# Moving the row sums, the roots and a weight staging inside the slots of a quantised attention stage

## What is computed

```python
x_int = x_int - jnp.max(x_int, axis=-1, keepdims=True)
x_int = jnp.maximum(x_int, n * x0_int)            # n = 30
q = jnp.floor(x_int / x0_int)
r = x_int - x0_int * q
z = r * (r + b_int) + c_int
exp_int = jnp.maximum(jnp.floor(z * jnp.exp2(n - q)), 0.0)
exp_sum = jnp.sum(exp_int, axis=-1, keepdims=True)
ratio = jnp.round(exp_sum / jnp.maximum(exp_int, 1.0))
big = jnp.floor(jnp.log2(ratio))
big = big + jnp.where(ratio - jnp.exp2(big) >= jnp.exp2(big - 1.0), 1.0, 0.0)
out = jnp.exp2(-jnp.clip(big, 0.0, qmax - 1.0))
```

## Time and profile before

| what | value |
|---|---|
| median of three runs | 658.2 us |
| the profiled execution, its own time | 656.87 us |
| its span in the profile | 655.1 us |
| DVE busy | 535.2 us, 82% of the span |
| ACT busy | 443.7 us, 68% |
| POOL busy | 402.9 us, 62% |
| PE busy | 369.4 us, 56% |
| attention slots 0 to 24 | about 74 to 413 us of the span |

### The profile page before, as it was taken

How to read it: one execution, slowest core, us unless ns; L and a number is a source line. 1 busy time by engine, 2 the same in 40 slices (tenths; PEclk the granted TensorE clock), 3 DMA queues, 4 the chain that set the end, 5 groups by cost and what they waited for, 6 DMA issues and landing times.

```text
span 655.1 us, 13415 instructions
## 1 busy us (share of the span) xinstructions
PE 369.4 (56%) x3593; PEld 236.0 (36%) x3593; DVE 535.2 (82%) x1380; ACT 443.7 (68%) x782; POOL 402.9 (62%) x450
## 2 busy tenths in 40 slices
PE   0598254072452633534536221278979999999264
PEld 0144112031130311312313111256757777777153
DVE  3688699679898897798998989669769998988566
ACT  0046657478767677677686765376878899998753
POOL 9773433431546487586785885477777777777600
PEclk9999555555555555555555555578989999999679
DMA  8546997786959969743422432466467776682098
GB/s 196 67 64 179 366 279 154 257 250 209 304 124 335 226 205 324 154 102 85 114 53 61 101 73 64 107 147 135 116 142 141 124 136 137 137 143 60 14 390 306
DMA packets 191976, 107.76 MB, mean 164 GB/s; under 512 B 137746, under 2 KB 186011, under 8 KB 191906
## 3 DMA queue, kind: packets, MB, share of 16 engines
q1 hardware_dynamic: 181634, 89.22, 56.2%
q0 software_dynamic: 10272, 17.70, 8.8%
HBM read 23.61 MB, written 60.67 MB: 129 GB/s over the span
## 4 chain that ended last, share of the span: by engine, by line
PE 27%; DVE 23%; SPq 13%; issue 13%; DMA 12%; ACT 8%; POOL 2%; DVEq 0%; POOLq 0%; ACTq 0%
PE pS L1925 8%; DMA pTs<-S_p 5%; PE pP L1925 5%; SPq L523 5%; PE pX L1943 4%; DVE S_e L1497 3%; DVE negmx L1422 3%; PE pO L1943 3%; SPq L611 2%; DMA w2s<-expert_rows 2%; SPq L514 2%; PE pS L1666 2%; DMA arena<-in_x_dram 2%; PE pS L1668 2%; DMA bias_rows_hl<-bias_hl 2%
## 5 line engine op out<-in xcount | busy, mean ns | idle before, releaser
L836 POOL DMA_INDIRECT expert_rows<-stage,dest x118 | 124.0, 1051 | 37.3 <-issue 29.6
L765 POOL DMA_INDIRECT region<-rows,slots x60 | 73.7, 1228 | 23.5 <-issue 16.3
L758 POOL CAST arena<-arena 128x384 bf16<-128x384 int8 x42 | 27.0, 643 | 70.0 <-ACT arena L926 69.3
L1843 PE MATMUL pP<-WpT,oq 128*128 128x192 bf16 x72 | 15.9, 359 | 74.0 <-ACT oq L1025 69.2
L1710 PE MATMUL pX<-arena,WA 128*128 128x384 f16 x86 | 34.9, 509 | 39.1 <-ACT arena L926 28.2
L765 POOL DMA_INDIRECT region<-arena,slots x36 | 45.5, 1265 | 18.4 <-issue 11.2
L926 ACT ACTIVATE arena<-pX,qkB,qkA 128x384 int8<-128x384 f32 x43 | 28.4, 661 | 41.6 <-PE pX L1710 41.6
L664 POOL TENSOR_TENSOR w1s<-stage,w1s 128x768 f16<-128x768 f32 (+1 forms) x16 | 33.8, 2113 | 32.9 <-ACT w2s L912 32.3
L1856 PE MATMUL pO<-pTs,vq 88*32 88x96 bf16 (+1 forms) x576 | 12.5, 238 | 71.5 <-DMA pTs<-S_p 71.3
L1497 DVE SCALAR_TENSOR_TENSOR S_e<-S_sq,kf,S_pow 128x1056 f32<-128x1056 f32 x24 | 38.2, 1591 | 16.7 <-ACT S_sq L1039 16.6
L1011 ACT ACTIVATE S_g<-S_w,kf 128x1056 int16<-128x1056 uint16 x24 | 30.3, 1264 | 27.7 <-DVE S_w L1427 27.7
(11 more groups left out here) (428 smaller groups left out, 1434.6 us busy)
## 6 DMA issues: line engine op xcount, KB each, us to landing
region<-zrow SPq DMA_DIRECT2D x11, 3200.0 KB, 12.2
w1s<-expert_rows SPq DMA_DIRECT2D x16, 384.0 KB, 8.0
stage<-in_L_ffn_w_dram SPq DMA_DIRECT2D x16, 192.0 KB
stage<-in_L_ffn_w_dram SPq DMA_DIRECT2D x32, 96.0 KB
w2s<-expert_rows SPq DMA_DIRECT2D x8, 384.0 KB, 11.7
arena<-in_x_dram SPq DMA_DIRECT2D x4, 672.0 KB
expert_rows<-stage,dest POOLq DMA_INDIRECT x118
out_dram<-xsel SPq DMA_DIRECT2D x8, 198.0 KB
```

Source lines behind the costliest of these rows:

```text
L765: pool.indirect_dma_start(region_rows, bass.IndirectOffsetOnAxis(ap=slots[q % 3][:, i, m:m + 1], axis=0), rows[q % 3][:, i, :].bitcast(I16 ...
L836: pool.indirect_dma_start(y_dram, bass.IndirectOffsetOnAxis(ap=dest[(st - 7) % 8][:, j:j + 1], axis=0), ysb[b][:, j, :], None, bounds_chec ...
```

## The change

On DVE the exponentials S_e of tile n - 1 stand at the head of slot n, followed by `top_experts` of the slot before and the maximum of tile n, and their sums stand behind that maximum. On ACT the root and its square stand together at the head of slot n and are written to a new tile S_y; the square over S_rho stands ahead of `scale_pair` and `split_pair`. The ratio reads S_y. Semaphores and their counts follow.

```diff
+        S_y = sb("S_y", [128, H, KEEP], F32)
...
@@ ACT, slot @@
+                if 1 <= st <= NT:
+                    act.wait_ge(s["e_ready"], n)
+                    if st >= 2:
+                        act.wait_ge(s["ratio_ready"], n - 1)
+                    act.activation(S_y[:, :, :], S_e[:, :, :], ACT.Abs_reciprocal_sqrt,
+                                   bias=k(K_TINY)).then_inc(s["inv_root"], 1)
+                    act.wait_ge(s["inv_root"], n)
+                    act.activation(S_y[:, :, :], S_y[:, :, :], ACT.Square).then_inc(s["y_ready"], 1)
                 if st < NT:
...
                     quant_qk(q + 1, 3, fill(st, "qk", 3))
+                if st < NT:
+
+                    act.wait_ge(s["rho_ready"], n + 1)
+                    if st >= 1:
+                        act.wait_ge(s["e_ready"], n)
+                    act.activation(S_sq[:, :, :], S_rho[:, :, :], ACT.Square, bias=k(K_NB2)).then_inc(s["sq_ready"], 1)
                 if i == 2 and st <= 20:
                     scale_pair(q + 1)
                 if i == 0 and 3 <= st < NT:
                     split_pair(q)
-                if st < NT:
-
-                    act.wait_ge(s["rho_ready"], n + 1)
-                    if st >= 1:
-                        act.wait_ge(s["ratio_ready"], n)
-                    act.activation(S_sq[:, :, :], S_rho[:, :, :], ACT.Square, bias=k(K_NB2)).then_inc(s["sq_ready"], 1)
...
-                if st < NT:
-
-                    act.wait_ge(s["e_ready"], n + 1)
-                    act.activation(S_sq[:, :, :], S_e[:, :, :], ACT.Abs_reciprocal_sqrt,
-                                   bias=k(K_TINY)).then_inc(s["inv_root"], 1)
                 if nxt and i < 2:
                     quant_qk(q + 1, 5 * i, fill(st, "qk", 5 * i))
-                if st < NT:
-                    act.wait_ge(s["inv_root"], n + 1)
-                    act.activation(S_sq[:, :, :], S_sq[:, :, :], ACT.Square).then_inc(s["y_ready"], 1)
...
@@ DVE, slot @@
+                if 1 <= st <= NT:
+
+                    dve.wait_ge(s["sq_ready"], n)
+                    dve.wait_ge(s["pow_ready"], n)
+                    dve.wait_ge(s["inv_root"], n - 1)
+                    dve.wait_ge(s["sum_ready"], n - 1)
+                    dve.scalar_tensor_tensor(S_e[:, :, :], S_sq[:, :, :], k(K_KK), S_pow[:, :, :].bitcast(BF16), ALU.add,
+                                             ALU.mult).then_inc(s["e_ready"], 1)
+                if 0 < st <= NT and quad_at(st - 1, GATE) is not None:
+                    top_experts(quad_at(st - 1, GATE))
                 if st < NT:
                     dve.wait_ge(s["u_ready"], n + 1)
                     dve.wait_ge(s["w_ready"], n)
                     dve.tensor_reduce(negmx[:, :], S_u[:, :, :], AX, ALU.max, negate=True).then_inc(s["max_ready"], 1)
+                if 1 <= st <= NT:
+                    dve.wait_ge(s["e_ready"], n)
+                    dve.wait_ge(s["ratio_ready"], n - 1)
+                    dve.tensor_reduce(esum[:, :], S_e[:, :, :], AX, ALU.add).then_inc(s["sum_ready"], 1)
+                if st < NT:
...
-                                             S_sq[:, :, :], ALU.max, ALU.mult).then_inc(s["ratio_ready"], 1)
+                                             S_y[:, :, :], ALU.max, ALU.mult).then_inc(s["ratio_ready"], 1)
...
-                if st < NT:
-
-                    dve.wait_ge(s["sq_ready"], n + 1)
-                    dve.wait_ge(s["pow_ready"], n + 1)
-                    dve.wait_ge(s["inv_root"], n)
-                    dve.wait_ge(s["sum_ready"], n)
-                    dve.scalar_tensor_tensor(S_e[:, :, :], S_sq[:, :, :], k(K_KK), S_pow[:, :, :].bitcast(BF16), ALU.add,
-                                             ALU.mult).then_inc(s["e_ready"], 1)
-                    dve.wait_ge(s["e_ready"], n + 1)
-                    dve.wait_ge(s["ratio_ready"], n)
-                    dve.tensor_reduce(esum[:, :], S_e[:, :, :], AX, ALU.add).then_inc(s["sum_ready"], 1)
-                if quad_at(st, GATE) is not None:
+                if quad_at(st, GATE) is not None and st >= NT:
                     top_experts(quad_at(st, GATE))
```

## The result

The changed kernel takes **664.1 us**, the median of four runs (660.65, 663.52, 664.68, 666.13), against 657.42 for the kernel before (median of four). The ratio is 1.0094, with a 95% interval of 1.0063 to 1.0125: 0.9% slower, some 6 us, where 657.2 was forecast. The profiled execution of the kernel after is its fastest, 660.65 (span 658.9 us), 3.8 over the one of before; the medians lie 6.7 apart.

The account below looks back on a forecast made before the run. DVE work and waits up to the low halves, and DVE work behind the gate's copy, were taken to bound the attention stage. Shifts summed to −1.0 on the profiled 656.87: 655.9, with 1.3 to the median 657.2; range 652.0 to 664.0.

Parts of the forecast that it names:

- Gains 1 and 2: Square ahead of staging ends DVE's wait before S_e (0.65 to 1.23); S_e clear of POOL's subtraction saves 0.42 to 0.87.
- the copy's old wait W: DVE's wait for the gate's copy in slots 7, 10, 13: 0.71, 1.12, 1.46, taken to vanish.
- The walk: Slot-by-slot sum of DVE's shift against before, from +2.45 at slot 1's ratio to −1.0 with the end's 1.65.
- S + 1.0 − W: Slots 7, 10, 13: new shift from DVE's shift S; S_e 1.2 later, sum 1.25 gone before copy, 1.06 behind it.
- Cost 1: Sum behind the gate's copy: maximum to S_w grows by 1.06 in six slots (7, 10, ..., 22).
- Gain 3: DVE's waits on itself: no dependent neighbours in the new order, 0.22 less a slot.
- Cost 2: Root behind the drain of qk0: ratio and S_g 1.2 later in slots 4, 7, 10 and 13.
- Cost 3: ACT's table loads: load plus root 2.45 in slot 0, and 1.65 at the end before the last ratio.
- dear loads: Rival: table loads also flush ACT, adding 1.38 to each of three, estimate 661.3; chance 0.04.
- the gate stays late: Slower rival: transposes asked earlier bring nothing, six quads each pay 1.06; 666.7, half of it 662; chance 0.20.
- DMA takes up the delays: Faster rival: saturated queues land work when they did, absorbing delays in slot 1 and quads 7, 10, 13; 653.3; chance 0.25.

Follow-up runs that it names:

- zero fill: Kernel after with POOL's subtraction in low_pair replaced by a memset of the same outputs to zero (low halves of expert weights left out); 0.9994 of the kernel before.

## Why the prediction was wrong

With the staging behind the square in all four, the two other parts give this square of ratios (the one in italics is from the slower session):

| | root at the slot's end | root at the next slot's head |
|---|---|---|
| sum behind S_e | 0.9972 | *0.9995* |
| sum behind the maximum | 1.0044 | 1.0094 |

The sum's move costs 0.7% with the root in its old place (1.0044 less 0.9972), the root's 0.5% with the sum in its new one (1.0094 less 1.0044), and the staging gives 0.2 to 0.3%. Taken in this order they make up the 0.9%. They do not simply add: with the sum in its old place the root's costs 0.2% (0.9995 less 0.9972), if the two sessions may be compared.

**The first step that failed is Gains 1 and 2 with their costing of the later staging at nothing.** The prediction asked only whether S_e gets clear of POOL, and whether the row normalisation on ACT comes in time. It did not ask what DVE does at the subtraction's new time. The waits fell (16.7 to 6.9, some 9 forecast), S_e took 1.3, and DVE was 2 us ahead in each i = 1 slot. But then S_w took 1.35 more and the second low half 0.71 more in six slots, 12.4 us, against the 11.3 that the two gains summed to. Two pairs of kernels differ by the staging alone from before and from after: with it moved, the one is 0.2% faster (0.9979), the other 0.1% slower (1.0066 against 1.0052). The zero fill shows that it is POOL's subtraction.

**The second is a term of the sum: that the copy's old wait W goes in slots 7, 10 and 13.** The walk has S + 1.0 − W there. The copy went on waiting 0.98, 1.07 and 1.42. Here are, in us behind S_w of the i = 2 slot before, the time at which P is finished, at which its DMA is issued, and at which the copy starts:

| slot | 7 | 10 | 13 | 16 | 19 | 22 |
|---|---|---|---|---|---|---|
| P finished, before | 29.5 | 29.8 | 33.0 | 31.3 | 31.3 | 29.7 |
| P finished, after | 30.7 | 31.3 | 32.4 | 31.0 | 31.0 | 29.5 |
| P's DMA, before | 33.0 | 33.7 | 36.0 | 32.6 | 32.6 | 31.3 |
| P's DMA, after | 33.1 | 33.8 | 34.7 | 32.3 | 32.3 | 31.1 |
| P's DMA, zero fill | 32.5 | 33.1 | 34.1 | 29.8 | 29.8 | 28.5 |
| copy, before | 37.9 | 38.6 | 42.2 | 39.2 | 39.3 | 36.3 |
| copy, after | 38.1 | 38.8 | 40.2 | 37.4 | 38.5 | 36.1 |
| copy, zero fill | 38.2 | 38.6 | 40.4 | 36.0 | 35.5 | 33.7 |

In these three kernels P's DMA always follows 0.1 behind the issue of the three turning DMAs. In slots 16, 19 and 22 that issue takes 3.8; there the longer S_w and low half take the gain away, and the zero fill gives it back. In slots 7, 10 and 13 the issue takes 5.8 to 8.8, and from the kernel after to the zero fill it begins 2.5 earlier, but P's DMA comes only 0.6 or 0.7 earlier and the copy moves by 0.2 at most. In slots 7 and 10, where 3.5 us of the miss lie, they did not move against the kernel before either, so DVE's gain was worth nothing there and the sum behind the copy counted in full. Ahead of slots 7, 10 and 13 a share of the region is still zeroed, ahead of the other three none is; that the zeroing is what holds the issue was not tested.

**Cost 1 was right in size and too narrow.** Root held back, sum moved or not: over the i = 1 slots, S_w to S_w, the kernel with only the root back needs 117.4 us in six quads and the one with both back 110.7, so 6.7 for the sum, against 6.4. (The two profiled executions lie 2.4 and 3.4 over the medians of their kernels.) The agreement is in the sum only: the slots differ by −0.4 to 2.3, and 1.4 of it is S_w, which takes 2.67 with the sum moved and 2.43 without. **Gain 3 was half right.** In the i = 0 slots (S_w to S_w up to i = 1) the sum's move gives 1.5 in six, 0.26 each, a little more than 0.22. In the five i = 2 slots from 8 on it gives 1.2, but only 0.1 each in slots 11, 14 and 17. There S_rho came to stand beside POOL's own low halves of the rows, 2.47 instead of 1.30, here in slot 11 of the kernel after:

```profile
235.11 0.71 POOL L343 TENSOR_TENSOR arena<-arena 128x192 f16<-128x192 f32 x1
235.78 0.90 POOL L344 TENSOR_TENSOR arena<-arena 128x384 f16<-128x384 f32 x1
```

```profile
235.33 2.47 DVE L1477 SCALAR_TENSOR_TENSOR S_rho<-S_g,kf,S_w 128x1056 int16<-128x1056 int16 x1
```

Together, 6.7 less 1.5 less 1.2 is 4.0 us, and 0.7% is 4.7.

**Cost 2** was right in direction: the root's place costs 3.3 us by the ratios, 1.7 of it at the end (**Cost 3**, forecast 1.65). The forecast 2.45 in slot 1 was 1.6. The 1.2 forecast for slots 7, 10 and 13 stood in the ratio's wait, as counted, but cost nothing: with the root back those slots take 61.8 us together, with it moved 61.7, since P's DMA waits for its turn in the queue anyway. The *dear loads* did not come: the second load starts at 408.03 and the root at 409.32, 1.29 later. The Trainium skill ("ScalarE: Activation LUTs", "What ACT_TABLE_LOAD costs") has 2.66 for it; these rows disagree again.

**The rivals.** What came is close to *the gate stays late* at half its price (662): against its quad's entry the copy moved up by less than 1.06 in four of six slots (−0.3, −0.2, 2.0, 1.8, 0.8, 0.2; S_w of the i = 2 slot before to the copy). Its reason was given as zeroing or P in the queue. In slots 7 and 10 it is the queue, as the table shows; in slots 19 and 22 nothing is zeroed any more, and there S_w and the low half are longer ahead of the DMAs. That the total came out near this rival's half price is luck in part, since two causes make it up. *DMA takes up the delays* did not come.

**The signs named** as "wrong" were S_e still beside POOL (it was not), copies of slots 16 and 19 not two us nearer to their quad's start (1.8 and 0.8: a miss), and a ratio in 16 or 19 that waits (it did not). The ratio's wait in slot 13, forecast at 4 or more, was 1.82, since the work ahead of it had become longer.

## What to carry to other kernels

Where DVE and POOL both do arithmetic with two inputs in SBUF, moving a POOL job in time can cost elsewhere what it frees here: lay the new span of that job over DVE's timeline and price each instruction under it, not only the one that got free. A reduction is a good thing to stand in a wait that will be there anyway; before moving one out of such a wait, check that the wait will close. Here it did not, because the queue of DMAs ahead of it set its end. Work that is done earlier is worth nothing where an issue in a queue takes longer by as much. And two reorderings that look like one edit should be forecast and measured each by itself: here one was worth keeping and two were not.

## What the runs showed of the hardware

**DVE beside POOL.** With two tensor inputs, S_w took 1.32 alone and 2.43 to 2.67 beside POOL's f32 subtraction of w1s, S_rho 1.30 and 2.47 beside POOL's low halves, the second low half 0.55 and 1.26. Beside a fill with zeros S_w kept 1.31, and the reductions, maximum and sum, stayed at 1.24 to 1.25 beside the subtraction too. The Trainium skill ("SBUF — State Buffer", "SBUF: two separate sides") says that a DVE operation with two SBUF inputs and a GpSimd operation that reads SBUF take turns, the one that starts first holding a shared pair of ports to its end. S_w of slot 13 in the kernel after fits. POOL's part of the subtraction on 64 rows, from its timeline:

```profile
254.50 1.63 POOL L665 TENSOR_TENSOR w1s<-stage,w1s 64x768 f16<-64x768 f32 x1
```

S_w started 0.08 behind it; 1.55 of waiting and 1.31 of work are 2.86, and 2.67 were measured. The order turned round is there as well. S_w in the earlier trace rows started at 252.81, as POOL's first part of the w2s subtraction ended (251.91 and 0.91), and took 1.32. POOL's second part started behind it and took 2.01; in the kernel after such a part takes 1.02 on average:

```profile
252.90 2.01 POOL L664 TENSOR_TENSOR w2s<-stage,w2s 64x384 f16<-64x384 f32 x1
```

In these rows a collision costs the engine that comes second. Beside S_w that was POOL in the kernel before, and its next job then still waited 1.97 for ACT; the move of the staging made it DVE.

**The issue of turning DMAs.** The three of a quad took 3.8 us to issue in slots 16, 19 and 22 of the kernel before, the kernel after and the zero fill, and 5.8 to 8.8 in slots 7, 10 and 13. Asked for 2.5 earlier, in slot 10 with the zero fill, they took 8.80 instead of 6.94.
